# A decoder layer on one core: the eight looped steps of the attention written out with constant waits

## What is computed

```python
x = _layernorm(x + mixer(x))                       # projection, short convolution, linear scan, gate, projection
x = _layernorm(x + attention(x, ctx_1024))         # 16 heads of width 16, softmax(q k / 4) v, projection
x = _layernorm(x + experts(x))                     # top-1 routing to 8 experts of capacity 640, relu MLP
```

## Time and profile before

| | us |
|---|---|
| runs: median (lowest to highest of 3) | 976.9 (973.17 to 978.64) |
| the profiled execution | 973.87 |
| its span | 972.1 |
| mean granted TensorE clock | 0.918 of full speed |

### The profile page before, as it was taken

One profiled execution on the slowest core, in us unless ns is written; L12 is line 12 of the kernel. 1 busy time (PEld: TensorE's weight loads), 2 busy tenths in 40 slices (PEclk: granted clock), 3 DMA queues, 4 the chain that ended last, 5 costly groups with the idle time before them and its releaser, 6 DMA issues. The chain is left out here.

```text
span 972.1 us, 16867 instructions
## 1 busy us (share of the span) xinstructions
PE 805.2 (83%) x5933; PEld 635.1 (65%) x5933; DVE 594.3 (61%) x1410; ACT 404.9 (42%) x639; POOL 356.3 (37%) x290
## 2 busy tenths in 40 slices
PE   5999955568998888899888887885299999999993
PEld 4777734345666666666656665543299999999993
DVE  4879854444578776777877766643255555555542
ACT  4565621123555554455455545551243233423320
POOL 0333434212254444455354444223222344235422
PEclk9999988767999999999999999875599999999997
DMA  4116401553554454464455434100533332233100
GB/s 121 44 45 201 131 19 60 127 136 94 125 132 130 114 156 136 125 157 119 115 136 157 130 111 131 55 21 21 177 96 101 115 108 98 91 114 120 38 27 18
DMA packets 75913, 100.91 MB, mean 104 GB/s; under 512 B 10961, under 2 KB 63354, under 8 KB 75856
## 3 DMA queue, kind: packets, MB, share of 16 engines
q1 hardware_dynamic: 72400, 92.03, 34.0%
q0 software_dynamic: 3456, 8.13, 2.3%
HBM read 65.47 MB, written 35.74 MB: 104 GB/s over the span
## 5 line engine op out<-in xcount | busy, mean ns | idle before, releaser
L971 DVE TENSOR_REDUCE nmax<-ps_m 128x4 f32<-128x1024 f32 x128 | 156.7, 1224 | 117.5 <-PE ps_m L732 114.7
L925 ACT ACTIVATE pt<-ps_a 128x1024 f32<-128x1024 f32 x128 | 131.1, 1024 | 138.0 <-PE ps_a L742 136.6
L1238 ACT ACTIVATE hid<-ps_h 128x640 fp32r<-128x640 f32 x64 | 45.1, 705 | 151.3 <-PE ps_h L1178 151.3
L1178 PE MATMUL ps_h<-xt,w_hi 128*128 128x320 f32 x512 | 100.0, 318 | 1.0 <-DVE xt L1253 1.0
L732 PE MATMUL ps_m<-kst,qst 48*128 48x256 f32 x512 | 68.7, 349 | 33.7 <-DMA qst<-halves_dram 30.1
L732 PEld LDWEIGHTS ps_m<-kst,qst 48*128 48x128 f32 x512 | 41.2, 199 | 77.8 <-issue 35.6
L1287 DVE SCALAR_TENSOR_TENSOR hid<-ps_h,hid 128x640 fp32r<-128x640 f32 x64 | 52.8, 825 | 56.1 <-ACT hid L1238 55.6
L1190 PE MATMUL ps_y<-w_hi,hid 128*128 128x256 f32 x640 | 85.3, 284 | 1.7 <-issue 1.7
L1178 PEld LDWEIGHTS ps_h<-xt,w_hi 128*128 128x128 f32 x512 | 80.1, 191 | 5.5 <-DVE hid L1287 3.3
L1190 PEld LDWEIGHTS ps_y<-w_hi,hid 128*128 128x128 f32 x640 | 80.1, 191 | 1.9 <-issue 1.9
L166 POOL TENSOR_TENSOR gated<-xh,sgate 128x512 f32<-128x512 f32 x32 | 42.2, 1319 | 88.1 <-ACT xh L259 88.1
(11 more groups left out here) (169 smaller groups left out, 1623.9 us busy)
## 6 DMA issues: line engine op xcount, KB each, us to landing
halves_dram<-half SPq DMA_DIRECT2D x64, 256.0 KB, 2.5
gated<-in_w SPq DMA_DIRECT2D x16, 1024.0 KB, 5.5
kst<-halves_dram SPq DMA_DIRECT2D x64, 128.0 KB, 3.2
qst<-halves_dram SPq DMA_DIRECT2D x64, 128.0 KB, 3.2
rows_dram<-blank SPq DMA_DIRECT2D x1, 5160.0 KB, 19.2
gated<-rows_dram SPq DMA_DIRECT2D x8, 645.0 KB, 4.2
x_raw<-in_x_t SPq DMA_DIRECT2D x8, 512.0 KB, 3.8
xres<-in_x SPq DMA_DIRECT2D x16, 256.0 KB, 3.8
```

The source lines that it names most:

```text
L925: nc.scalar.activation(pt[:, k % 4].rearrange("p s t q -> p (s t q)"), ps_a[:].rearrange("p s t q -> p (s t q)"), ACT.Exp).then_inc(s["exp ...
L971: nc.vector.tensor_reduce(nmax[:, q, :, :, h // 2].rearrange("p t s -> p s t"), ps_m[:], AX.X, ALU.max, negate=True).then_inc(s["max_done" ...
L1178: mm = pe.matmul(ps_h[:, f % 2, c2, 0:HC], w1[a][:, p, k, f * P:(f + 1) * P], xt[:, b, p, k, c2 * HC:(c2 + 1) * HC], start=(n == 0 and k = ...
L1238: nc.scalar.activation(hid[:, HI, f, :].rearrange("p (c n) -> p c n", c=2), ps_h[:, f % 2, :, 0:HC], ACT.Relu).then_inc(s["hid_hi"], 1)
```

## The change

`run` calls every step with a Python number. The hardware loop of steps 6 to 13 is gone, and with it the registers, the branches and the register forms of waits and addresses. The order of the instructions that do work is the same on every engine. `FIRST` and `LAST` are used nowhere else. Lines behind L470 move up by 7.

```diff
@@ -467,16 +467,9 @@
-    FIRST, LAST = 6, B - 3
-
     def run(eng, step):
 
-        for n in range(-1, FIRST):
-            step(n, n % 2)
-        with eng.Fori(0, (LAST + 1 - FIRST) // 2) as i:
-            step(i * 2 + FIRST, FIRST % 2)
-            step(i * 2 + FIRST + 1, (FIRST + 1) % 2)
-        for n in range(LAST + 1, B + 4):
+        for n in range(-1, B + 4):
             step(n, n % 2)
```

## The result

| | before | written out |
|---|---|---|
| median | 975.09 us | 979.83 us |
| runs | 20 (967.57 to 978.64, and one of 1099.75) | 20 (973.23 to 985.07) |
| ratio to before, 95% interval | | 1.0051 (1.003 to 1.0072) |
| profiled execution | 973.87 us | 977.08 us |
| its span and mean clock | 972.1 us, 0.918 | 975.2 us, 0.919 |

The written-out kernel is about half a per cent slower. The run of 1099.75 us counts as slow and is left out of the ratio. Forecast were 979.3 us, a rise of 2.4; measured are 979.83 and a rise of 4.7, with 2.9 to 7.0 in the interval. In the profiled execution it is 3.2.

The account below looks back on a forecast made before the run. Each step was taken as a chain through PE, the fullest engine, and the engines it waits for. Steps +1.6 and clock +0.8 on the 976.9 us median gave 979.3 us, range 974 to 986.

Parts of the forecast that it names:

- the hold: VectorE's L1007 takes 1.19 instead of 0.17 us when GpSimd's L623 starts 0.11 ahead; 0.57 reaches PE.
- The pattern of steps 4, 5 and 14: Steps already written out show the new form: 28.17 us a step, against 27.95 for a looped one.
- the entry to the loop: VectorE's entry at the end of step 5 makes that step 0.1 to 0.2 us too long as a pattern.
- What the registers cost: Loop's register instructions and branch: removal saves 0.55 us in an odd step, 0.14 in an even, mean about 0.35.
- what they hide: GpSimd's register instruction delays L623 past L1007; without it all eight L1007 lose 1.02 us, 0.57 of it on PE.
- the back part: From PE's L776 to the next step: 5.66 us in odd step 9, 5.11 in written-out step 4, saving 0.55.
- the front part: From step start to PE's L776: 22.44 us in looped step 9, 23.01 in written-out step 4.
- The sum for steps 6 to 13: Eight steps of 28.17, 225.4 in place of 223.6 us, less 0.2 for the loop's entry: +1.6.
- The clock: Falls from 2.4 to 1.2 GHz cost 1.66 us each; half a further fall was added, 0.8 us.
- The rival that named PE's longer wait at the count: Clock falls more often: a fall in every step gives 986.8 us; two or more further falls, chance 0.19.
- The first rival: In steps 6 to 13 L1007 starts first, unheld: step 27.55, change -3.4 us, 973.5 us; chance 0.08.
- Instruction loading: Some 9 more blocks on q8; the rival has PE wait about 1 us at each, 988 us; chance 0.03.

Follow-up runs that it names:

- loop_held: Kernel before, with the loop, plus two waits on constant, long-reached counts ahead of VectorE's L1007: 974.92 us, ratio 0.9994.
- loop_dve_op: Kernel before, with the loop, plus a one-value-per-partition fill of a spare tile on VectorE ahead of L1007: 976.86 us, ratio 1.001.
- flat_late1: Written-out kernel plus one wait on a constant, long-reached count on GpSimd after its wait for x1: 980.43 us in one timed run.
- flat_late3: Written-out kernel plus three waits on constant, long-reached counts on GpSimd after its wait for x1: 978.84 us, ratio 1.0043.
- flat_pool_op: Written-out kernel plus a one-value-per-partition fill of a spare tile on GpSimd ahead of L616: 979.8 us, ratio 1.0031.
- loop_twice: Kernel before, with the loop, with VectorE's L1007 done twice, first into a spare tile: 990.08 us, ratio 1.0148.
- flat_mv_first: Written-out kernel with VectorE's mean and variance for L1000 taken ahead of x1: 967.98 us, ratio 0.9911.
- loop_qfirst: Kernel before, with the loop, with PE's queries ahead of the count that waits for the one-hot rows: 968.96 us, ratio 0.9925.
- the two edits: Written-out kernel with PE's queries ahead of the count and VectorE's mean and variance ahead of x1: 960.11 us, ratio 0.9839.

## Why the prediction was right, and where it was short

**The time and the rise.** The time came out 0.5 us above the forecast, and that is in part luck. The forecast stood on 976.9, the median of three runs, and the kernel before has 975.09 in twenty. That base was 1.8 too high, and the rise of 4.7 was forecast at half its size, 2.4; the two errors nearly cancel. What held is the mechanism: the direction, both parts of the sum and the place of the hold.

**The pattern of steps 4, 5 and 14.** It held: 28.17 was taken for a written-out step, 28.15 is its length in steps 7, 10, 11 and 13. That the entry to the loop lengthened step 5 held too (28.30 to 28.14).

**What the registers cost, and what they hide.** Both halves are read in the trace of the kernel after, and the hold is shown by itself in the experiments. L1067 to L971 went from 0.56 to 0.08, the back part from 5.66 to 5.10; L1007 went from 0.17 to 1.19 in all eight steps, and the front part from 22.44 to 23.06. I put the hold at 0.57 on PE's path. Taking it away by one edit measured 0.63 in the flat kernel, putting it into the loop 0.87 in an odd step, the extra operation included.

**The sum for steps 6 to 13.** +1.6 forecast, +2.3 found with the falls taken off at 1.66 each, of which 0.7 are the two longer steps 8 and 9. The pattern had neither of their causes.

**The clock, the term that was most mis-sized.** I gave it half a fall, 0.8 us. The profiled execution of the written-out kernel had one fall fewer in steps 6 to 13 than that of before, yet the medians rose by 4.7. More profiles of each kind tell why one is not enough. Windows of steps 6 to 13, first of two loop kernels whose edits moved nothing (loop_held, loop_dve_op):

```profile
324.83:553.68 228.85, 205.33 (x1700) 144.75 (x1690) 170.07 (x457) 119.70 (x210) 105.86 (x96) 0.97 0.50 133
```

```profile
324.41:552.94 228.53, 203.46 (x1688) 144.16 (x1688) 172.52 (x466) 119.38 (x208) 105.64 (x96) 0.98 0.49 134
```

and of three flat ones that kept their hold (flat_late1, flat_late3, flat_pool_op):

```profile
322.98:555.03 232.05, 205.71 (x1692) 145.00 (x1688) 170.84 (x457) 120.46 (x209) 104.43 (x96) 0.97 0.47 132
```

```profile
323.43:555.50 232.07, 205.69 (x1688) 144.84 (x1688) 170.84 (x457) 120.51 (x208) 104.41 (x96) 0.97 0.47 133
```

```profile
323.39:556.67 233.28, 207.00 (x1688) 145.28 (x1688) 171.22 (x457) 119.77 (x208) 104.84 (x104) 0.96 0.47 132
```

With the kernel before and the one after that is 228.6, 228.9, 228.5 against 229.2, 232.1, 232.1 and 233.3, a mean difference of 3.0 us. The clock fell 3, 4 and 3 times in the loops and 2, 4, 4 and 5 times in the flat ones, so a profile of one kind can have more falls than one of the other, and seven profiles do not settle the number.

More runs say more. Each run has a mean granted clock on record: it is 0.9152 over 44 runs of the flat kernel with its hold (the kernel after, flat_late3, flat_pool_op) and 0.9171 over 88 of the loop (the kernel before beside the experiments, loop_held, loop_dve_op). Their mean spans are 977.7 and 973.8 us. If the lower clock is always 0.5, that is 165.8 us at half clock against 161.4; at 1.66 per 3.4 us the difference costs an estimated 2.1 us, give or take 1.3 by the spread of the runs. The other 1.8 of the 3.9 lies with the steps, near the 1.6 forecast. So the clock took some 1.3 falls where half a fall was put, and this is the larger part of what the forecast lacks. The rest of the 4.7 lies within the interval.

Why the clock falls more often is not settled. The rival that named PE's longer wait at the count points the right way. Falls in the flat kernels mostly come right behind it, 9.5 to 10.1 into steps 4, 6 and 12 of the profile after. In loop_twice, where the hold sits on top of the loop's costs, seven of eight steps had one, and flat_mv_first, without the hold, has a mean clock of 0.9190. Against it stands loop_qfirst, in which PE does not wait at the count at all: its clock is 0.9156, and it fell in four of the eight steps. Its condition was two or more further falls; the average of 1.3 is below that, though the spread reaches it.

**The first rival**, that the hold does not come, fell in this kernel, but flat_mv_first is that case made by hand: a step of 27.52 against the 27.55 worked out. Its change was put at -3.4 us and is -8.2 against the kernel before beside it (967.98 and 976.21), since four more steps (4, 5, 14 and 15) lose their hold as well, some 2.4, and the falls get fewer.

**Instruction loading.** Ten more blocks on q8 (44 against 34) for about nine forecast, and no stall of about 1 us in a step: PE's waits in step 7 are those of step 4 before. The one candidate is VectorE's pause of 0.28 in step 9, which every written-out kernel has at the same instruction; no run tests whether it comes from loading. That a taken branch to a target outside what is held forces a fetch (the Trainium skill, "Runtime: NRT & Kernel Launch", section "Instruction fetch mechanics") no run here shows, since the loop ran on 1 block in 182 us. The branch did cost VectorE 0.5 a turn; it was smaller than what it hid.

## What to carry to other kernels

A loop that has written-out turns beside it carries its own forecast: cut the trace at the same instruction in both kinds of turn, and read which instruction got longer, not only which are gone. If an operation takes many times its usual length in one form only, look at what the other engine starts within about 0.1 us of it; here a register instruction kept two engines from meeting, and its removal cost more than the loop had. Turn such a race on purpose, by another order on one engine or by taking the waiting work off the path, and remove the loop then: alone that lost 0.5%, with the two edits the kernel, written out, gained 1.6%.

## What was not expected of the hardware

- Waits on constants that are long reached cost nothing in front of an operation that waits for something later: three of them moved GpSimd's start by less than 0.01 us. They were passed 1.5 us ahead of the start in the first step.
- A tie is not a hold. With both starts within 0.02 us, VectorE's operation took 0.17 and GpSimd's 1.29 to 1.31 against 1.27, and that was so in the odd steps of loop_dve_op too, where GpSimd started 4 to 6 ns ahead; with GpSimd 0.06 to 0.07 ahead, VectorE's took 1.25.
- The clock's falls can come at a fixed pace: in flat_late1 and flat_late3 it fell in every second step from 4 to 14, with steps of 28.15 and 29.78 in turn. In the kernel after and in flat_pool_op, with steps of nearly the same lengths, it did not. What decides it is not shown.
